# Macaron attention layer on one core: the last score tile of a slot goes behind the last max tile on TensorE

## The reference, cut to what matters

```
x = x + 0.5 * ffn(layernorm(x))        # stage a
x = x + attention(layernorm(x))        # qkv at the end of stage a, attention in stage b
x = x + 0.5 * ffn(layernorm(x))        # stage c

# attention, 16 heads of 16 features
scores = einsum('bhqd,bhkd->bhqk', q / 4, k)
scores = where(pos_q >= pos_k, scores, -inf)
out    = softmax(scores) @ v, then the output projection
```

## Time and profile before

| | us |
|---|---|
| median of 3 runs | 1429.2 |
| lowest and highest | 1426.5, 1436.69 |
| profiled execution | 1427.34 |
| its span in the trace | 1425.6 |
| stage b, first to last transpose (31 group lengths) | 332.2 to 1163.3 |
| PE busy | 1301.0 |
| DVE busy | 1177.4 |
| ACT busy | 908.6 |

### The profile page before, as it was taken

One profiled execution on the slowest core, in us unless ns is written; L12 is line 12 of the kernel. 1 busy time (PEld: TensorE's weight loads), 2 busy tenths in 40 slices (PEclk: granted clock), 3 DMA queues, 4 the chain that ended last, 5 costly groups with the idle time before them and its releaser, 6 DMA issues. The chain is left out here.

```text
span 1425.6 us, 38170 instructions
## 1 busy us (share of the span) xinstructions
PE 1301.0 (91%) x9260; PEld 831.4 (58%) x9260; DVE 1177.4 (83%) x4599; ACT 908.6 (64%) x1828; POOL 458.7 (32%) x877
## 2 busy tenths in 40 slices
PE   3999999979999999999999999999999995988885
PEld 3999889845444444444444444444444443877875
DVE  4788888758899999999999999999999982778786
ACT  3666666613777777777777777777777774444442
POOL 3333433211122222222222222122123123877772
PEclk9999999975999999999999999999999997998898
DMA  3466556943456456456356456456456444444441
GB/s 107 156 233 230 206 207 219 265 174 53 69 98 105 68 100 102 68 98 103 69 100 102 69 102 100 69 101 101 69 103 98 69 99 135 151 157 162 155 154 60
DMA packets 121898, 174.11 MB, mean 122 GB/s; under 512 B 44012, under 2 KB 71788, under 8 KB 121804
## 3 DMA queue, kind: packets, MB, share of 16 engines
q1 hardware_dynamic: 121816, 173.30, 52.1%
HBM read 96.08 MB, written 76.02 MB: 121 GB/s over the span
## 5 line engine op out<-in xcount | busy, mean ns | idle before, releaser
L973 ACT ACTIVATE b_probs<-bank 128x512 f32<-128x512 f32 x1152 | 595.3, 606 | 183.4 <-PE bank L1095 182.9
L1006 DVE CUSTOM_DVE_ANT_0 b_junk<-bank,mask 128x512 bf16<-128x512 f32 (+3 forms) x1032 | 447.9, 489 | 7.5 <-issue 7.5
L1009 DVE TENSOR_REDUCE b_pm<-bank 128x1 f32<-128x512 f32 x516 | 319.7, 683 | 28.4 <-PE bank L1077 28.4
L1077 PE MATMUL bank<-ks,qs 48*128 48x512 f32 (+3 forms) x1056 | 325.8, 409 | 7.2 <-PEq L435 6.3
L1095 PE MATMUL bank<-qs,ks 50*128 50x512 f32 (+3 forms) x1056 | 301.0, 389 | 20.2 <-ACT b_probs L973 13.4
L1111 PE MATMUL bank<-b_probs,b_vx 128*32 128x512 f32 (+3 forms) x3072 | 310.6, 500 | 3.1 <-POOL b_probs L941 2.0
L1095 PEld LDWEIGHTS bank<-qs,ks 50*128 50x128 f32 x1056 | 164.8, 189 | 214.2 <-ACT b_probs L973 196.8
L137 POOL TENSOR_TENSOR hold_pool<-zero 128x1 f32<-128x1 f32 x192 | 37.2, 194 | 675.4 <-ACT b_probs L973 675.3
L1077 PEld LDWEIGHTS bank<-ks,qs 48*128 48x128 f32 x1056 | 172.3, 195 | 54.6 <-DVE b_pm L1006 24.2
L941 POOL TENSOR_SCALAR_AFFINE_SELECT b_probs<-b_probs 128x512 f32<-128x512 f32 x256 | 158.3, 637 | 0.0
L1095 PE MATMUL bank<-b_qs,b_ks 50*128 50x512 f32 (+3 forms) x480 | 137.1, 382 | 9.7 <-ACT b_probs L973 6.5
(11 more groups left out here) (104 smaller groups left out, 2077.2 us busy)
## 6 DMA issues: line engine op xcount, KB each, us to landing
scr_qk<-a_qk SPq DMA_DIRECT2D x64, 512.0 KB, 3.2
qs<-scr_qk SPq DMA_DIRECT2D x132, 128.0 KB, 4.4
ks<-scr_qk SPq DMA_DIRECT2D x132, 128.0 KB, 4.9
scr_o<-b_o SPq DMA_DIRECT2D x64, 256.0 KB, 2.3
b_qs<-scr_qk SPq DMA_DIRECT2D x66, 128.0 KB, 4.0
b_ks<-scr_qk SPq DMA_DIRECT2D x66, 128.0 KB, 4.5
a_x<-x SPq DMA_DIRECT2D x16, 512.0 KB, 3.5
scr_x<-a_x SPq DMA_DIRECT2D x16, 512.0 KB, 2.7
```

The lines of the kernel that those rows point to most:

```text
L973: act.activation(probs[:, s % NBUF, h, :], score_bank(t, last)[:], ACT.Exp).then_inc(p_ready, 1)
L1006: ins = dve.tensor_tensor_reduce(junk[:, t % SB, off:off + w], src, mask[:, BANK - w:BANK], 1.0, 0.0, ALU.add, ALU.max, pm[:, g.buf, 0, pl ...
L1009: ins = dve.tensor_reduce(pm[:, g.buf, 1, place(h), i:i + 1], src, AX.X, ALU.max)
L1077: last = pe.matmul(m_bank[t % SB][:, off:off + w], qs[g.buf][rows(h, SROWS), h // 2, i * P:(i + 1) * P], ks[g.buf][rows(h, SROWS), h // 2, ...
```

## The change

Inside a slot, only the first score tile still goes ahead of its max tile. In the three pairs behind it the max tile goes first. M_ORDER is (1, 0, 3, 2) in place of (1, 3, 0, 2), for PE and DVE alike. The order in a slot becomes

```diff
-S_ORDER, M_ORDER = (0, 2, 1, 3), (1, 3, 0, 2)
+S_ORDER, M_ORDER = (0, 2, 1, 3), (1, 0, 3, 2)
...
             def step(g, last):
                 for s in range(NSLOT):
                     for h in range(GH):
-                        score_tile(g, s, h, last)
+                        if h == 0:
+                            score_tile(g, s, h, last)
                         if s == NSLOT - AHEAD + 1 and h == 0 and not last:
                             turn_m(g.next(1))
                         if not last:
...
                                 max_tile(g.next(1), a, h)
                             else:
                                 max_tile(g.next(2), a - NSLOT, h)
+                        if h > 0:
+                            score_tile(g, s, h, last)
                     if s >= 2:
                         values(g, s - 2)
```

## The result

The changed kernel takes 1448.15 us (median of 4 runs, 1443.62 to 1450.55) against 1429.15 of the kernel before: a ratio of 1.0119, 95% interval 1.0078 to 1.016. It is slower, clear of the noise though by less than 2%: by 19 us where 31 were forecast. Its profiled execution took 1446.87 us, with a span of 1445.1.

The account below looks back on a forecast made before the run. The bound was the slot's cycle of M1, its maximum, the release, M2's drain and the values, 2.72 us. Later values add 1.00 us in each of 31 groups: 1427.3 + 31 = 1458.3, said as 1458; range 1429 to 1468.

Parts of the forecast that it names:

- M2 gains nothing: Last pair of a slot: M2 is let go by DVE later than S3 by ACT; gain taken as 0, at most 9 us.
- S3 behind it makes the values late: End of a slot: values start later by S3's lag behind M2, 0.10 us, or 0.20 in slots 3 to 5.
- The first rival: End of a slot: S3 is taken in while M2 waits, both start together; 2.5 us, 1430 in all; chance 0.24.
- the prediction's walk around the group: Stage b: ends of six slots add 0.10 each, two add 0.20, slot 5 none; 1.00 us a group.
- d: End of a slot: S3's start behind M2; 0.10 us behind one piece, 0.20 behind two, upper end 0.13 and 0.26.
- The sum: Whole kernel: 1427.3 us of the profiled execution plus 31 gives 1458.3, forecast as 1458 us.
- The thinnest cover: ACT's idle in slot 7: second exponential slips 0.4 to 0.5 us; cost 0 to 0.1 a group, taken as 0.
- PE can pass a tile that waits for its half: Tiles ahead of M2: no loss from shared halves; the opposite, 6 to 9 us more, 1467, had chance 0.08.

Follow-up runs that it names:

- one-slot kernels: Kernel before with the last score and max tile exchanged in slot 5 alone, or in slot 4 alone: 1423.64 and 1441.3 us, groups 26.69 and 26.82 us.
- kernels with early values: Values moved ahead of the fourth pair: in the kernel before 1418.61 us, ratio 0.9923; in the changed kernel 1471.2 us profiled, group 28.02 us.
- split kernel: Kernel before with the values in two halves, one on each side of the fourth pair: 1408.44 us, ratio 0.9822, group 25.27 us.

## Why the prediction was right, and where it was not

**The mechanism.** The prediction said that M2 gains nothing and that S3 behind it makes the values late. Both are shown: M2 loads 0.05 to 0.06 behind the end of the maximum in each of 154 slots of the kernel before and 151 of the changed one, and swapping the last pair alone gives 27.41 us a group, the inner pairs and the heads 26.69 and 26.68. The first rival (S3 taken in while M2 is held) is refuted by S3's 0.08 to 0.09 in each of 249 tails.

**Which delays count.** By the prediction's walk around the group eight of nine tails lengthen it and that of slot 5 doesn't. The two one-slot kernels bear out the two tails where that was close, 26.69 and 26.82. The walk with the measured terms: 0.08 to 0.09 in each of slots 7, 8, 0, 1, 2, 3 and 6, and 0.14 in slot 4, is 0.73.

**The term that was mis-sized.** The step was d = 0.20 behind an M2 in two pieces. It was taken from a held tile with two tiles behind it, on the ground that as many instructions lie between. But there the middle tile shared the half of the held one and its load came 0.11 behind, so half of the 0.20 was, as I read it now, that wait; behind M2's first piece PE issues S3's load 0.09 later, ahead of the second piece. Slots 3 and 4 were put at 0.40 and measured 0.22. d = 0.10 in one piece was 0.09, and made the values 0.08 late. So 0.73 in place of 1.00 a group, 22.6 in place of 31 us.

**What the profile of before hid.** The sum was made on an execution whose first two groups took 57.33 us. The changed kernel's took 53.99, where two groups longer by 0.73 each would have made 58.79. That is another 4.8 us, and luck of the clock rather than the change's making: the kernel with only the heads changed had 32.30 and 32.79 in its profiled execution and 1440.04 us, with steady groups of 26.68.

**What else moves.** The thinnest cover was named rightly. In slot 7 the second exponential comes late by M0's wait for the copied maxima, and ACT idles 0.31 us ahead of it, but slot 7 grew from 3.55 to 3.64 us, by the tail alone. That PE can pass a tile that waits for its half was right too: in the slot shown M3 starts at 723.77 and S2, which is earlier in the program and shares M0's half, at 724.01. Two such neighbours a slot cost nothing.

**A reading that was wrong.** The prediction reads 8 tenths for DVE from rows 1; from slice 12 to slice 32 they show 9. DVE was as full as PE by that measure. No term of the sum rests on it, since the timeline and not the busy share was used.

**What I didn't foresee** is that the same reasoning, used on the kernels with early values, needed the rotation of the banks as well: which tile is held follows from the number of tiles since the last values, not from its name.

## What to carry to other kernels

Ask of a wait who is let go last, not which sum is longest: here 260 us of waits for ACT were free, and clearing them away put a tile behind the one that was really held. In an in-order queue the tile that is held longest should stand last before a switch to an operation that needs the whole array, and if something must stand behind it, it should use the other half. The gain was in giving PE work for the time in which that tile is held, without letting the bank rotation wait for it.

## What the runs showed of the hardware

- Behind a max tile held for DVE, a score tile in the other half loads its weights 0.09 us later (0.08 to 0.09 in 249 tails of the changed kernel), and one in the same half starts 0.33 to 0.34 later. Where the first isn't held they start within 0.01 (slots 7, 8, 0, 1, 2, 4 and 5 of the split kernel with the last pair swapped). The Trainium skill (TensorE: Matmul & The Clock Gate, Architectural detail) has PE pull weight loads ahead of running matmuls; no load was pulled ahead of a held one in the slots read here.
- The clock was the larger risk. Kernels whose group was 25.3 to 28.0 us long ran stage b at 2.4 GHz in their profiles, but for its beginning and for one run of the split kernel with the last pair swapped. With 28.02 us a group two of four runs were far above (1581.36 and 1648.41), with 29.5 and 28.8 the clock was at 1.2 GHz for most of the stage: 45.03 and 44.27 us a group. Windows of the kernel with two score tiles behind M2, either side of a fall:

```profile
680.00:700.00 20.00, 17.37 (x135) 8.68 (x138) 16.53 (x67) 14.04 (x27) 6.35 (x15) 1.00 0.73 118
700.00:720.00 20.00, 19.25 (x96) 7.19 (x88) 12.63 (x46) 11.20 (x22) 1.55 (x4) 0.68 0.37 72
```

PE was busy for 17.37 of the 20 us ahead of it. The two kernels with a group 2.8 and 2.2 us longer took 30 and 32% more time, not the 6 or 5% that the group at 2.4 GHz would give. The length of the group alone doesn't settle it, since one run of the split kernel with the last pair swapped had 1.2 GHz through stage b, and that kernel's group is 25.36 us at 2.4 GHz. Why the same program fell in one run and not in another stays open.
